# A second copy, in PSUM, of the rounded part of each short embedding table

## The reference: what is computed

```python
e = jnp.stack([tbl_0[ids[:, 0]], ..., tbl_25[ids[:, 25]]], axis=1)
z = concatenate([dense, einsum('bnd,bmd->bnm', all27, all27)[upper triangle]], axis=1)
h = concatenate([z, dense], axis=1)
h = maximum(h @ W_top1 + b_top1, 0); h = maximum(h @ W_top2 + b_top2, 0)
y = h @ W_top3
```

## Time and profile before

| | |
|---|---|
| median of 3 runs | 477.35 us (477.17 to 479.39) |
| the profiled execution | 478.75 us, its span 477.0 us |
| PE | busy 417.5 us (88% of the span) |
| PEld | 393.0 us (82%) |
| DVE | 338.8 us (71%) |
| ACT | 215.8 us (45%) |
| POOL | 399.8 us (84%) |

### The profile page before, as it was taken

How to read it: one execution, slowest core, us unless ns; L and a number is a source line. 1 busy time by engine, 2 the same in 40 slices (tenths; PEclk the granted TensorE clock), 3 DMA queues, 4 the chain that set the end, 5 groups by cost and what they waited for, 6 DMA issues and landing times.

```text
span 477.0 us, 11689 instructions
## 1 busy us (share of the span) xinstructions
PE 417.5 (88%) x4198; PEld 393.0 (82%) x4198; DVE 338.8 (71%) x777; ACT 215.8 (45%) x719; POOL 399.8 (84%) x553
## 2 busy tenths in 40 slices
PE   0546796979999999999999959999699969999796
PEld 0446696979999999899999959999698969899685
DVE  3659869798598769886897648875587848855060
ACT  1054254454545545545553624554254453545251
POOL 7999989989899898898998989989898988989300
PEclk9958788899999999999999979999899998999899
DMA  7973422622132222123223313222222213131000
GB/s 182 232 199 106 113 51 76 166 70 80 47 84 53 72 73 78 47 74 81 56 64 76 81 39 85 55 78 63 46 78 74 83 39 85 40 78 39 23 2 0
DMA packets 19682, 36.58 MB, mean 77 GB/s; under 512 B 7823, under 2 KB 10391, under 8 KB 19630
## 3 DMA queue, kind: packets, MB, share of 16 engines
q0 software_dynamic: 8704, 17.84, 16.6%
q1 hardware_dynamic: 10926, 18.04, 13.0%
HBM read 35.85 MB, written 0.01 MB: 75 GB/s over the span
## 4 chain that ended last, share of the span: by engine, by line
POOL 64%; issue 27%; PE 4%; ACT 2%; POOLq 1%; DMA 1%; DVE 0%; ACTq 0%; DVEq 0%
POOL rows L402 36%; POOL y_wide L391 28%; PE mlp_ps L500 2%; PE mlp_ps L509 1%; ACT inter L648 1%; POOLq L390 1%; DMA rows<-in_tbl,idx_sb 1%; PE dots_ps L461 0%; DVE inter L811 0%; DMA idx_sb<-in_ids 0%; PE mlp_ps L516 0%; PE late_ps L437 0%; ACT x_hi L657 0%; ACT h_sb L664 0%; ACT h_sb L671 0%
## 5 line engine op out<-in xcount | busy, mean ns | idle before, releaser
L402 POOL DMA_INDIRECT rows<-in_tbl,idx_sb x272 | 265.8, 977 | 45.6 <-POOL y_wide L391 43.8
L763 DVE TENSOR_TENSOR onehot<-ids_sb,late_ps 125x1024 fp32r<-125x1024 int32 (+2 forms) x154 | 167.8, 1142 | 12.6 <-DMA ids_sb<-in_ids_by_round 6.4
L811 DVE COPY_PREDICATED inter<-mask,dots_ps 27x48 f32<-27x48 int32 x496 | 103.1, 208 | 60.4 <-ACT inter L648 45.7
L391 POOL MEMSET y_wide<- 64x448 f32 x272 | 133.8, 492 | 0.2
L648 ACT COPY inter<-dots_ps 27x64 f32<-27x64 f32 x496 | 99.0, 200 | 59.1 <-PE dots_ps L461 47.8
L461 PE MATMUL dots_ps<-vecs 128*64 128x54 f32 x1984 | 118.7, 226 | 1.5 <-ACT vecs L624 0.9
L461 PEld LDWEIGHTS dots_ps<-vecs 128*64 128x64 f32 x1984 | 114.7, 140 | 6.0 <-issue 2.4
L477 PE MATMUL turn_ps<-onehot,t_hi 125*128 125x256 f32 x378 | 101.1, 304 | 10.3 <-DVE vecs L604 10.3
L477 PE MATMUL turn_ps<-onehot,t_lo 125*128 125x256 f32 x378 | 96.5, 291 | 0.0
L477 PEld LDWEIGHTS turn_ps<-onehot,t_hi 125*128 125x128 f32 x378 | 75.8, 200 | 14.8 <-issue 8.5
L477 PE MATMUL late_ps<-onehot,t_hi 125*128 125x256 f32 x214 | 59.7, 312 | 21.1 <-DVE t_lo L776 16.6
(11 more groups left out here) (52 smaller groups left out, 353.3 us busy)
## 6 DMA issues: line engine op xcount, KB each, us to landing
ids_sb<-in_ids_by_round SPq DMA_DIRECT2D x25, 375.0 KB
rows<-in_tbl,idx_sb POOLq DMA_INDIRECT x272, 2.6
vecs<-in_tbl SPq DMA_DIRECT2D x8, 448.0 KB
rows<-in_r_dense_features SPq DMA_DIRECT2D x16, 64.0 KB, 5.2
h_sb<-in_W_top_laid SPq DMA_DIRECT2D x2, 512.0 KB, 18.3
vecs<-in_tbl SPq DMA_DIRECT2D x1, 560.0 KB
w_sb<-in_W_top SPq DMA_DIRECT2D x1, 512.0 KB
vecs<-in_tbl SPq DMA_DIRECT2D x8, 52.0 KB
```

What stands on the lines that cost most here:

```text
L391: pool.memset(unread, 0.0).then_inc(pauses_made, 1)
L402: nc.gpsimd.indirect_dma_start(out=rows[v % 2][:, s, :], out_offset=None, in_=tables[f - 1][:, :], in_offset=bass.IndirectOffsetOnAxis(ap= ...
L763: dve.tensor_tensor(part_buffer(k, h)[0:KP, 0:n], home.rearrange("p (o r) -> p o r", o=1).to_broadcast([KP, n, R]), row_of[KT[k]][0:KP, a: ...
L811: dve.copy_predicated(inter_of(u, q, g, a, n), mask[g * 32:g * 32 + N, a:a + n].rearrange("p (j s) -> p j s", s=1).to_broadcast([N, n, QS] ...
```

## The change

For each of the eight short tables ACT reads the rounded part again, as soon as it stands in SBUF, and writes it into `dots_ps`, which is idle at that time. DVE waits for this copy (`hi_shown`) in place of the rounded part in SBUF, and subtracts with the copy as second operand. There is one place for the copy, so `show(n)` waits until DVE's split(n - 1) is done. The ninth table and the weights are split as before. In ACT's queue `show(0)` stands behind `split(2)`, and `show(n + 1)` ahead of `copy_fetched(n)`.

```diff
+    SHORTS = KT.index(LONG)
+        def shown(n):
+            return dots_ps[0:KP].rearrange("p s c -> p (s c)")
@@ scalar
+            def show(n):
+                act.wait_ge(hi_made, split_count(n))
+                if n:
+                    act.wait_ge(lo_made, split_count(n - 1))
+                nc.scalar.copy(shown(n), piece(n, True).bitcast(F32)).then_inc(hi_shown, 1)
...
                     for n in range(3):
                         split(n)
+                    show(0)
                     act.wait_ge(pads_zero, 1)
                     zero_pads(0)
                     for n in range(X):
+                        if n + 1 < SHORTS:
+                            show(n + 1)
                         copy_fetched(0, -1, n)
@@ vector
             def split(n):
-                dve.wait_ge(hi_made, split_count(n))
-                dve.tensor_tensor(piece(n, False), staged_piece(n), piece(n, True).bitcast(F32),
+                if n < SHORTS:
+                    dve.wait_ge(hi_shown, n + 1)
+                else:
+                    dve.wait_ge(hi_made, split_count(n))
+                dve.tensor_tensor(piece(n, False), staged_piece(n),
+                                  shown(n) if n < SHORTS else piece(n, True).bitcast(F32),
                                   ALU.subtract).then_inc(lo_made, 1)
```

More of the change, by code:

```diff
@@ L165, in dlrm_tower @@
         hi_made = sem("hi_made")
+        hi_shown = sem("hi_shown")
         lo_made = sem("lo_made")
```

## The result

The changed kernel takes 481.69 us (median; 480.73 to 484.61) against 477.5 us before: ratio 1.0095, 95% interval 1.0076 to 1.0114. It is slower by about 4 us. The forecast was 477.4 us and a range up to 480.2. Timed a second time, beside the experiments, the same kernel gave 480.04 us and a ratio of 1.0069 (1.0048 to 1.0090), so the size to explain is 2.4 to 4.2 us by the medians (the kernel before had 477.68 that time) and 3.3 to 4.5 by the ratios. The profiled execution took 482.3 us, its span 480.6 us. That of the kernel before took 478.75, about 1 us above its medians, so that differences of spans from it come out about 1 us too small.

What follows compares the result with a forecast made beforehand. It took POOL's gathers and pauses to bound the kernel; a 4.2 us gain would be spent waiting for PE's transposes (1.8 us at tile 2, 2.3 at tile 4), net 0.0, so 477.4 us, range 474.4 to 480.2.

Steps and rivals of the forecast that it cites:

- What bounds the kernel: Whole run: POOL's gathers and pauses set the time; PE's smallest room is 8.4 us, at tile 4.
- SP's late loads: SP's queue at the start: ninth table, first weights and other loads go at 33.6 instead of about 18, costed at nothing.
- What POOL gains: Before tile 2: gathers no longer stall under eight table subtractions, gaining 4.2 to 4.6 us, taken as 4.2.
- The memset: Near 15 us: DVE's memset might still hold the gather at 14.96, leaving it 0.4 us late.
- Durations: At the start: ACT's copy from SBUF into PSUM takes 1.05 us (bounds 0.6 and 1.3), DVE's subtraction with PSUM operand 1.22.
- The order at the start: First 52 us: show(0) waits behind split(2), DVE's split(2) begins at 37.5, fetch(5) at 52.0, 8.4 us late.
- So the other six copies lie beside compares and cost nothing.: ACT's later copies at the start: each shown before DVE asks, about 1 us of room, otherwise 1.05 us each.
- the rival in which ACT sets the pace: At the start: shows 3 to 7 each 0.7 us late, delay 11.9, end +3.5, 480.9 us; chance 0.20.
- End = before + (delay of PE at tile 2 - 8.4).: POOL's wait at tile 4: PE's delay beyond 8.4 us of room lengthens the run, gain at most 2.4 us.
- Delay of PE at tile 2 8.4.: Tile 2's transposes: PE 8.4 us late, ending at 118.3; bounds 5.6 to 10.5.
- the half clock: PE at 55.40 to 62.20: without it PE regains about 2.8 us; fetch(5) slow from its start raises the delay.
- Behind tile 4 I took the rest as fixed: After tile 4: tiles 5 and 6 have more room than 8.4 us, PE's 15.9 us of waits absorb its delay.

Runs made afterwards that it cites:

- PE late alone: The kernel before, no copies, with 110 idle transposes on PE ahead of the first dot products: 481.99 us, ratio 1.0103; with 55: 477.7 us, ratio 1.0007.
- the early order and the PSUM operand: The changed kernel with ACT's show(0) and show(1) moved ahead of split(2), subtraction still reading the PSUM copy: 477.1 us, ratio 0.9974.
- second profile: The changed kernel profiled again, unedited, beside the later experiments: 480.04 us, ratio 1.0069.
- order alone: The kernel before without any copy, DVE's split(0) and split(1) made to wait until ACT's split(2) is done: 477.37 us, ratio 0.9986.
- early, SBUF: The changed kernel with show(0) and show(1) ahead of split(2), and DVE subtracting with the rounded part in SBUF, copies kept: 480.6 us, ratio 1.0048.

## Why the prediction was wrong

- **What bounds the kernel.** Right. POOL's account adds up to the last gather in every kernel, and with PE late alone POOL waits at tile 4, where the forecast had the nearest point. SP's late loads, costed at nothing, cost POOL nothing that shows: its waits end with the transposes.
- **What POOL gains.** Right: 5.09 - 0.23 = 4.9 us, of which 0.28 is the ninth table's stall, which only moved (and grew to 0.78 at tile 2); the rest is 4.6, the upper bound, where I took 4.2. The memset does not hold a gather: with the early order and the PSUM operand, the gather at 14.88 took 0.95 with the memset of 14.92 to 15.40 beside it, and a subtraction that began at 15.32. Of the two things that the Trainium skill ("SBUF — State Buffer", section "Who interferes with whom") says, these gathers follow the rule for a GpSimd instruction that reads SBUF: they are held off, and 3.3 to 3.5 us of the whole kernel hang on it. They take their row numbers from SBUF (`idx_sb`); whether the writing of descriptors by itself would be held off, which the page infers it is not, no run here separates.
- **Durations.** Right: 1.01 to 1.06 us for a copy into PSUM (taken 1.05), 1.22 for the subtraction. The 62 cycles more for a PSUM source, by the Trainium skill ("VectorE: DVE Perf Modes", section on the TRN2 errata), are not in these rows.
- **The order at the start.** Right to within a microsecond up to fetch(5): 51.33 against 52.0, so 7.7 us late where the forecast had 8.4.
- **"So the other six copies lie beside compares and cost nothing."** This is the first step that failed. (The other copies are five, shows 3 to 7: by its own working show(2), which ends at 37.5, is on the path.) It holds for shows 3 to 6. Show(7) stands behind the copy of fetch(5), which waits for DVE's vectors, and behind the cast of the ninth table, longest of all; split(7) waits 1.4 us. I had the rival in which ACT sets the pace, but priced it for five copies at 0.7 each and at half clock, and did not follow the queue for each n. So this term, put at nothing, was 1.4 us on the path, and moving show(7) alone gave back 1.9 us of the median.
- **"End = before + (delay of PE at tile 2 - 8.4)."** This is the second step that failed: the wait was priced as if POOL went on the moment the transposes end. POOL starts 1.42 us behind the start of the last transposes, about 1.0 behind their end. The formula lacks this 1.0: the room was 7.4 us, not 8.4. In the second profile, where PE was 8.7 us late, it is most of what tile 4 lost: 8.7 - 7.4 = 1.3, measured 1.32. In the first it is 10.9 - 7.4 = 3.5, measured 3.48.
- **"Delay of PE at tile 2 8.4."** 8.7 in one execution, 10.9 in the other, with the half clock. The bounds named the half clock (up to 10.5), and the first profile lies beyond them. That the second comes so near 8.4 is luck: fetch(5) began 0.5 us less late than forecast, it and its copy's wait took 3.8 us (2.5 before; the clock was 0.50 in that stretch against 0.80), split(7) waited 1.4 us, so that tile 0's last transposes were 9.9 us late, and PE made up 1.2 by tile 2.
- **Behind tile 4 I took the rest as fixed.** The stalls there were 1.45 us before and 2.63 and 1.93 after; from the last gather to the end it is 1.0 us less (32.08 before, 31.04 and 31.08 after). The first profile adds up: 3.48 at tile 4, + 1.16 from there to the last gather, - 1.04 = 3.6 us, which is the difference of the spans. The second gives 1.32 + 0.48 - 1.00 = 0.8 us, with 2.4 in the medians. Single executions differ by as much as these terms, so that the medians are explained in kind and only roughly in size.

What stays open: why the kernel before has the smallest stalls behind tile 4. That gathers and subtractions keep a fixed phase to each other there, and that it fell well in that kernel, is argued from the table and not tested; with one execution of each kernel it can also be chance.

## What to carry to other kernels

When a change puts an instruction into a queue written by hand, follow that queue for every turn, and ask for each new instruction what the one ahead of it is waiting for; one copy of eight, taken to cost nothing, cost 1.9 us of a loss of 2.4 to 4.2. Before counting a gain on the engine that bounds the kernel, find the nearest point at which this engine must wait for another, and its room with both moved: earlier by the gain, later by the cost, and less the time from the event to the start of the work that waits for it. The room can be measured directly, by making the other engine late with idle work.

## What the runs showed of the hardware

- A gather of GpSimd that begins under or just ahead of a VectorE subtraction with two SBUF operands waits for it and ends about 0.82 us behind it: up to 2.4 us in place of 0.95. With one operand in PSUM it does not: over 0.95, all 34 gathers before tile 2 together took 5.09 us before and 0.23 after.
- A gather that had to wait for PE's transposes starts 1.0 us behind their end, twelve times of twelve at tiles 2 and 4, and also where they had ended 0.26 us before GpSimd was free. The first gather of tile 2 took 1.73 or 1.74 us in the five profiles with a wait there; in each it lies under the ninth table's subtraction and ends 0.82 or 0.83 us behind it, so that this is the stall again and no cost of the wait.
- What the stalls cost differs with the order alone: the same nine table subtractions in SBUF cost about 2.2 us (order alone) and 6.1 us (early, SBUF), the sums of the table less the 0.19 us of the very first gather, which is long in every kernel.
